# A longer lead loop in a two-layer attention and expert kernel: 16 more attention steps before the first expert tile, half A's post chain between its steps, expert scores computed token-major

## The reference, cut to what matters

```
x = x + tanh(g_xattn[0]) * attention0(layernorm(x), ctx)    # 16 heads of 16; 1024 queries x 1024 keys, quantized
x = x + tanh(g_ffn[0])   * experts0(layernorm(x))           # 32 experts of 176 units and a shared one of 352
x = x + tanh(g_xattn[1]) * attention1(layernorm(x), ctx)    # small
x = x + tanh(g_ffn[1])   * experts1(layernorm(x))           # 32 experts of 96 units, shared 192
```

```
scores = sigmoid(x @ router_weight.T)       # 32 experts
sfc = scores + e_bias                       # 8 groups of 4; the 4 groups whose two best sum highest stay
top 8 of what stays; combine = scores of those 8 / their sum * 2.5
```

## Time and profile before

| | |
|---|---|
| median of 3 runs | 980.28 us (980.24 to 982.89) |
| the profiled execution's own time | 977.45 us |
| its span in the profile | 975.7 us (1.75 us lie around it) |
| PE busy, weight loads, DVE, ACT, POOL | 878.6, 656.2, 760.2, 532.4, 574.2 us |
| mean granted PE clock | 0.948 |
| the chain that ended last | PE 65%, DVE 9%, POOL 6%, DMA 5%, issue 3%, ACT 3% |

### The profile page before, as it was taken

How to read it: one execution, slowest core, us unless ns; L and a number is a source line. 1 busy time by engine, 2 the same in 40 slices (tenths; PEclk the granted TensorE clock), 3 DMA queues, 4 the chain that set the end, 5 groups by cost and what they waited for, 6 DMA issues and landing times.

```text
span 975.7 us, 16764 instructions
## 1 busy us (share of the span) xinstructions
PE 878.6 (90%) x6100; PEld 656.2 (67%) x6100; DVE 760.2 (78%) x1058; ACT 532.4 (55%) x936; POOL 574.2 (59%) x500
## 2 busy tenths in 40 slices
PE   5627777877999999999899999999999999999997
PEld 4525445545777777777676777777776777777775
DVE  5998788665888888877777677878878767878886
ACT  4527777644666666655446645444446654343432
POOL 4433766655899898976586565444347554334341
PEclk9868788678999999999999999999999999999999
DMA  5006999832776666642222122323322112232320
GB/s 192 2 1 136 179 176 164 160 97 55 145 152 143 142 152 151 148 125 68 78 66 81 51 66 83 95 86 94 97 82 82 57 58 82 82 91 87 97 87 22
DMA packets 162083, 97.79 MB, mean 100 GB/s; under 512 B 138833, under 2 KB 142801, under 8 KB 162001
## 3 DMA queue, kind: packets, MB, share of 16 engines
q1 hardware_dynamic: 161728, 96.19, 40.2%
q10 hardware_dynamic: 272, 0.52, 0.1%
HBM read 62.08 MB, written 1.05 MB: 65 GB/s over the span
## 4 chain that ended last, share of the span: by engine, by line
PE 65%; DVE 9%; POOL 6%; DMA 5%; issue 3%; ACT 3%; DVEq 0%; SPq 0%; POOLq 0%; ACTq 0%
PE psum L226 19%; PE psum L228 18%; PE psum L227 18%; DMA pT<-p 5%; PE psum L736 3%; DVE qstack L1441 2%; ACT e L1036 2%; POOL p L1491 2%; POOL wlo L1499 2%; PE psum L907 1%; PE psum L746 1%; PE psum L747 1%; DVE qstack L1427 1%; PE psum L893 1%; DVE nmax L1185 1%
## 5 line engine op out<-in xcount | busy, mean ns | idle before, releaser
L1499 POOL TENSOR_TENSOR wlo<-wraw,whi 128x768 fp32r<-128x768 f32 x146 | 272.2, 1864 | 196.9 <-ACT whi L1046 194.9
L226 PE MATMUL psum<-actT_hi,whi 128*128 128x512 f32 x584 | 244.3, 418 | 4.0 <-issue 2.1
L1148 ACT ACTIVATE h_hi<-qstack 128x512 fp32r<-128x512 f32 x146 | 92.5, 633 | 260.6 <-DVE qstack L1441 244.2
L228 PE MATMUL psum<-actT_hi,wlo 128*128 128x512 f32 x584 | 233.0, 399 | 0.0
L227 PE MATMUL psum<-actT_lo,whi 128*128 128x512 f32 x584 | 232.7, 398 | 0.0
L1441 DVE TENSOR_TENSOR qstack<-qstack 128x512 f32<-128x512 f32 x136 | 184.5, 1357 | 12.5 <-DVE qstack L1427 0.5
L1491 POOL TENSOR_SCALAR p<-e 128x1024 f16<-128x1024 f32 x128 | 142.7, 1115 | 84.4 <-ACT e L1036 68.7
L1036 ACT ACTIVATE e<-psum,nmax 128x1024 f32<-128x1024 f32 x128 | 142.6, 1115 | 42.7 <-DVE nmax L1185 28.7
L1185 DVE TENSOR_REDUCE nmax<-psum 128x1 f32<-128x1024 f32 x128 | 152.8, 1216 | 14.7 <-PE psum L736 12.1
L1419 DVE SCALAR_TENSOR_TENSOR qstack<-qstack,psum 128x512 f32<-128x512 f32 x146 | 99.8, 684 | 66.0 <-ACT qstack L1111 65.4
L226 PEld LDWEIGHTS psum<-actT_hi,whi 128*128 128x128 f32 x584 | 111.0, 190 | 36.5 <-issue 6.2
(11 more groups left out here) (196 smaller groups left out, 1148.0 us busy)
## 6 DMA issues: line engine op xcount, KB each, us to landing
wraw<-in_wffn SPq DMA_DIRECT2D x146, 384.0 KB, 3.1
pT<-p SPq DMA_TRANSPOSE x128, 2.9
ctxT<-in_ctxT SPq DMA_DIRECT2D x2, 512.0 KB, 5.1
x<-in_x SPq DMA_DIRECT2D x1, 1024.0 KB, 8.5
ctok<-in_ctx SPq DMA_DIRECT2D x1, 1024.0 KB, 11.1
out<-x SPq DMA_DIRECT2D x4, 256.0 KB, 2.9
kstack<-in_Wkv ACTq DMA_DIRECT2D x1, 512.0 KB, 5.0
kstack<-in_Wq SPq DMA_DIRECT2D x1, 256.0 KB, 8.7
```

The source lines that it names most:

```text
L226: pe.matmul(out, l_hi, r_hi, start=start, stop=False, **kw)
L228: return pe.matmul(out, l_lo, r_hi, start=False, stop=stop, **kw)
L1499: pool.tensor_tensor(wlo[:, g % RING, :], wraw[:, g % RING, :], whi[:, g % RING, :].bitcast(F32), ALU.subtract).then_inc(cf["w_lo"], 1)
```

## The change

- The lead loop is 16 steps longer: `LEAD_OUT` = 80 steps are attended in it, `LEAD` = 84 are scored. There is no bridge.
- The post chain of half A's second unit stands between the loop's steps (70 to 82), like the first unit's. `weights_hi`/`weights_lo` for tiles 0 and 1 stand at s = 58 and 62.
- `paced()` starts at step 84 and puts two steps beside one tile of three and one beside the other two; `END0` becomes 38.
- `route(r)` makes its scores token-major for all four rounds: activations are now the stationary operand and the router's 32 columns the moving one, so there are 24 matmuls of 32 columns, each with a load of 128 columns. `route_sb`, `scores_transposed` and the copy out of PSUM go; tanh writes `score` and `score_in` works in place.
- `route0`'s part j of round 0 runs at the start of tile j on DVE, ahead of its s_g.
- `down(0)` waits for the tanh and for `osb`; `gate` of the first pass waits for exp of step 81.

```diff
-        LEAD = A_STEPS + LAG
-        BRIDGE = 4
+        LEAD_OUT = A_STEPS + HEADS0
+        LEAD = LEAD_OUT + LAG
...
-            s, out, j = LEAD + BRIDGE, LEAD + BRIDGE - LAG, QUIET
+            s, out, j = LEAD, LEAD_OUT, QUIET
             while out < STEPS:
-                n = 1 if j % 3 == 1 else 2
+                n = 2 if j % 3 == 0 else 1
...
                 def route(r):
                     pe.wait_ge(cp["x_lo"], 2 * r + 2)
-                    ps = bank(post_bank(r, 0, "route"))[0:EXPERTS, :]
-                    cut, layer = cols(r % 2), r // 2
-                    for k in range(KD):
-                        last = mm3(pe, ps, rw_hi[:, layer, k, :], rw_lo[:, layer, k, :], actT_hi[:, k, cut],
-                                   actT_lo[:, k, cut], start=k == 0, stop=k == KD - 1)
+                    ps, layer = bank(post_bank(r, 0, "route")), r // 2
+                    for t in range(TH):
+                        tt = slice((r % 2 * TH + t) * P, (r % 2 * TH + t + 1) * P)
+                        for k in range(KD):
+                            last = mm3(pe, ps[:, t * EXPERTS:(t + 1) * EXPERTS], actT_hi[:, k, tt], actT_lo[:, k, tt],
+                                       rw_hi[:, layer, k, :], rw_lo[:, layer, k, :], start=k == 0, stop=k == KD - 1)
...
                     if f == 0:
                         pe.wait_ge(c2["part"], made_before(j))
-                        pe.wait_ge(c2["exp"], LEAD)
+                        pe.wait_ge(c2["exp"], LEAD - 2)
...
                     if g == 0:
-                        pe.wait_ge(cp["score"], 1)
+                        pe.wait_ge(cp["route_sb"], 1)
+                        pe.wait_ge(c2["osb"], TH + 1)
...
-                    if s == 39:
-                        o_transposed(0, 0)
-                    elif s == 43:
-                        project(0, 0)
-                    elif s == 51:
-                        x_transposed(0, 0)
+                    if s in (39, 70):
+                        o_transposed(0, s > A_STEPS)
+                    elif s in (43, 73):
+                        project(0, s > A_STEPS)
+                    elif s in (51, 78):
+                        x_transposed(0, s > A_STEPS)
+                    elif s == 81:
+                        route(0)
...
 ACT
+                    if s in (40, 71):
+                        o_high(0, s > A_STEPS)
+                    elif s in (49, 77):
+                        norm_apply(act, ...)
+                    elif s in (52, 79):
+                        x_high(0, s > A_STEPS)
+                    elif s in (58, 62):
+                        weights_hi((s - 58) // 4)
+                    elif s == 82:
+                        route_act(0)
...
 DVE
+                    if s in (42, 73):
+                        o_low(0, s > A_STEPS)
+                    elif s in (46, 75):
+                        post_x(0, s > A_STEPS)
+                    elif s in (55, 81):
+                        x_low(0, s > A_STEPS)
+                out_lead(TH)
...
+                    if f == 0 and j < 3:
+                        route0(j, 0)
...
 POOL
+                    if s in (47, 75):
+                        norm_rstd(pool, ...)
+                    elif s in (58, 62):
+                        weights_lo((s - 58) // 4)
```

More of the change, by code:

```diff
@@ L613, in made_before @@
         def made_before(j):
-            return BRIDGE + sum(1 for i in AT if i < j and AT[i])
+            return sum(1 for i in AT if i < j and AT[i])
         def s_bank(s):
-            return 2 + 2 * (s % S_RING) if s < LEAD else 4 + 2 * ((s + 1) % 2)
+            return 2 + 2 * (s % S_RING) if s < LEAD else 4 + 2 * (s % 2)
         def s_user(s):
@@ L675, in post_bank @@
         def post_bank(r, u, stage):
-            return 1 if r == 0 else {"o": 4 + u, "y": 6 + u, "x": 4 + u, "route": 6, "score": 7}[stage]
+            return 1 if r == 0 else {"o": 4 + u, "y": 6 + u, "x": 4 + u, "route": 6}[stage]
         def tile_of(r, u):
@@ L704, in _ @@
                     load(g)
-                for s in range(LEAD + BRIDGE):
+                for s in range(LEAD):
                     turn(s)
@@ L902, in turn1 @@
                         pe.wait_ge(cx["pT_a"], n)
+                        if p == 0:
+                            pe.wait_ge(cp["route_sb"], half + 2)
                     else:
@@ L915, in attend1 @@
                     pe.wait_ge(cx["pT_d"], 2 * t + 2)
-                    if i == 0:
-                        pe.wait_ge(cp["score"], half + 2)
-                    else:
+                    if i > 0:
                         pe.wait_ge(cx["x"], t)
@@ L1001, in _ @@
                         attend(s - LAG, bank(0)[:, at:at + HD0])
-                o_transposed(0, 1)
-                scores(LEAD)
-                pe.wait_ge(c2["exp"], LEAD - 1)
-                attend_group([LEAD - LAG])
-                project(0, 1)
-                for i in range(1, BRIDGE):
-                    if i == BRIDGE - 1:
-                        x_transposed(0, 1)
-                    scores(LEAD + i)
-                    pe.wait_ge(c2["part"], i)
-                    attend_group([LEAD + i - LAG])
-                route(0)
                 for f in range(len(PASSES)):
@@ L1065, in route_act @@
                     act.wait_ge(cp["route_ps"], r + 1)
-                    act.activation(route_sb[0:EXPERTS, :], bank(post_bank(r, 0, "route"))[0:EXPERTS, :], ACT.Tanh,
-                                   scale=0.5).then_inc(cp["route_sb"], 1)
+                    if r > 0:
+                        act.wait_ge(cp["comb"], r)
+                    act.activation(score[:, :, :],
+                                   bank(post_bank(r, 0, "route"))[:, 0:TH * EXPERTS].rearrange("p (t e) -> p t e", t=TH),
+                                   ACT.Tanh, scale=0.5).then_inc(cp["route_sb"], 1)
                 def exp1(half, p):
@@ L1456, in _ @@
                         out_lead(s // HEADS0 - 1)
-                    if s == 42:
-                        o_low(0, 0)
-                    elif s == 46:
-                        post_x(0, 0)
-                    elif s == 54 + 1:
-                        x_low(0, 0)
-                out_lead(TH - 1)
-                row_max(LEAD)
-                o_low(0, 1)
-                out_group(GROUPS0[0][1])
-                row_max(LEAD + 1)
-                post_x(0, 1)
-                out_group(GROUPS0[1][1])
-                row_max(LEAD + 2)
-                out_group(GROUPS0[2][1])
-                x_low(0, 1)
-                row_max(LEAD + 3)
-                out_group(GROUPS0[3][1])
+                    if s in (42, 73):
[5 more added lines that the diff above has]
+                out_lead(TH)
                 for f in range(len(PASSES)):
@@ L1567, in _ @@
                     quantize(s)
-                    if s == 47:
-                        norm_rstd(pool, step, tile_of(0, 0), norm_at(0, 0), cn["stats"], cn["rstd"])
-                quantize(LEAD)
-                weights_lo(0)
-                quantize(LEAD + 1)
-                norm_rstd(pool, step, tile_of(0, 1), norm_at(0, 1), cn["stats"], cn["rstd"])
-                quantize(LEAD + 2)
-                weights_lo(1)
-                quantize(LEAD + 3)
+                    if s in (47, 75):
+                        norm_rstd(pool, step, tile_of(0, s > A_STEPS), norm_at(0, s > A_STEPS), cn["stats"], cn["rstd"])
+                    elif s in (58, 62):
+                        weights_lo((s - 58) // 4)
                 for f in range(len(PASSES)):
```

48 lines of the change are left out of this document (7 added, 41 removed).

## The result

The changed kernel takes 990.8 us (median of 5 runs, 987.65 to 993.97), the kernel before beside it 980.28 (979.28 to 982.89): ratio 1.0109, 95% interval 1.0083 to 1.0136. It is 1.1% slower. The forecast was 976.6, the range 971.0 to 984.0.

What follows compares the result with a forecast made beforehand. It took PE to bound the paced tiles, DMA to pace the lead loop, and waits to fill the bridge and tiles 0 to 2. Terms +8.4 - 9.9 - 5.3 + 3.1 = -3.7 us gave 976.6 us, range 971.0 to 984.0.

Steps and rivals of the forecast that it cites:

- Term 1: Lead loop against bridge: 16 more loop steps plus inserted work take 29.3 us instead of 20.9, +8.4 us.
- (a): Lead loop: route(0) ahead of attends 77 to 79, 2.8 us on PE, of which 0.8 exposed.
- (b): Lead loop: weight splits at s = 58 and 62 delay quantize; 3 us together with the second post chain.
- (c): Lead loop: tighter second post chain makes DVE wait 1 to 2.5 us; 3 us together with the weight splits.
- Term 2: Paced tiles: twelve steps fewer at 0.82 us of PE each, no other engine becoming the bound, -9.9 us.
- Term 3: Tiles 0 to 2: choice parts ahead of s_g, first gate to tile 3's 18.0 us instead of 23.3, -5.3 us.
- Term 4: Token-major scores in rounds 1 to 3: 24 matmuls in 2.8 us instead of 1.77, +3.1 us.
- rival C: Route matmuls: small moving operands don't hide the weight load, 4.6 us a route, 983.7 us; chance 0.12.
- B: Lead loop laid bare at post_x and weights_lo: inserts cost 12.6 us instead of 3, 986.2 us; chance 0.12.
- from 218 on: Sign at the lead loop's end: first gate matmul at 218 us or later, against about 213.9 forecast.
- the clock dropping in the longer loop: Lead loop sign of a wrong forecast: route and gate double in length at half speed.

Runs made afterwards that it cites:

- h1: The changed kernel with POOL's weights_lo behind h_lo in the paced tiles alone; 985.4 us, ratio 1.0049.
- e3: The kernel before with the weight splits of tiles 0 and 1 at s = 58 and 62 of the lead loop; 981.2 us, ratio 1.0031.
- e4: The changed kernel with the old form of the scores in all rounds; 983.6 us, ratio 1.0041.
- f2: The changed kernel with the eight unlift matmuls left out of each attend in the paced tiles, output wrong by the lift; 988.5 us, ratio 1.0084.
- f1: The kernel before with the choice's parts ahead of s_g in tiles 0 to 2, old scores; 979.6 us, ratio 1.0005.
- h2: e4 with a later second post chain, splits at steps 80 and 82, and weights_lo behind h_lo in the paced tiles alone; 975.7 us, ratio 0.9949.
- g2: The kernel before with POOL's order quantize, h_lo, weights_lo in all the first pass's tiles; 990.4 us, ratio 1.0103.
- e2: The kernel before with token-major scores and the choice's parts ahead of s_g in tiles 0 to 2; 991.5 us, ratio 1.0119.
- g1: The changed kernel with POOL's order quantize, h_lo, weights_lo in all the first pass's tiles; 997.7 us, ratio 1.0180.

## Why the prediction was wrong

The profiled execution came 16.5 us later where the sum said -3.7, a miss of 20.2 us; by the medians it is +10.5 and 14.2. The terms below are read from the two profiled executions and miss by 8.1, 5.5, 2.1 and 2.3 us; 1.7 are the later exp 0, and the rest lies between a gate and its s_g. Some 6 us of the 20.2 belong to these two executions and not to the kernels, the 1.7 among them; h1, with the same lead, was 4.0 us shorter from exp 67 to s_g 0.

**Term 1, the lead loop, is the step that failed most.** Up to the first gate the change costs 3.1 + 13.4 = 16.5 us, not 8.4. What was inserted cost 11.9 us for the 3.8 of the sum. (a) "I take 0.8 exposed" for `route(0)`, "2.8 the upper". It took 5.1 us, since the clock was at half there, and 4.5 of them were exposed. The price came from a row at the full clock for a stretch where the bridge shows 0.53. And the wait that was to hide it, "these attends wait for their transposes anyway", was over at 218.9 us, 1.5 us behind `route(0)`'s start. (b) and (c) "I take 3 us". The splits cost 2.3 to 3.1 and lie ahead of exp 67. The held-up transposes, which were to hide 2 to 3 us ("about 2", while its sum gives 3), hid little of them: two splits of 1.82 us cost 3.3 in e3. From exp 67 to exp 79 (212.25) it took 22.8 us where 12 steps of 1.54 are 18.5: 4.3 for the post chain, 3.8 of them at exp 76 (5.3 - 1.5; in e4, f2 and h1 it was 2.3). The chain's wait, foreseen as "1 to 2.5 us", was 2.64 of DVE's idle time, and `post_x` itself comes on top. The pace of 1.54 us for a step without inserts was right.

**Term 2, the paced tiles: "PE has no idle time there to swallow this" was wrong.** -4.4 came of the -9.9. A step was priced a little low, 0.82 us for 0.93 (17.20 less 16.28, one step). But with twelve steps fewer PE no longer bounds the stage: POOL's `weights_lo` against DVE's h does, by 0.62 us in three tiles. With POOL's order turned round the same twelve steps give -11.3 (205.9 to 194.6). The prediction named the lock for the choice alone, and h, at a mean of 1.64 us in the three tiles of the earlier trace rows, isn't among its rows. That row by itself would only have warned: in the kernel before, the stretched h cost nothing. The reading of the stage before, bound by PE, was right; that it would stay so was taken from the busy time of POOL and DVE, not from which of their operations stand ahead of s_g.

**Term 3, tiles 0 to 2:** -3.2 by the gates (20.1 for 23.3) instead of -5.3. The mechanism was right, with the race a tile later than foreseen: part 1's product, at the start of tile 1, met `weights_lo(3)`, began 0.01 us behind it and took 1.98 us. In h1 it was ahead, took 1.27 us, and tile 3's gate came 17.6 us behind tile 0's (17.2 from s_g to s_g). So the forecast's 17.2 and 19.0 were 17.6 and 20.1, the latter with PE's 1.11 us wait for the weights on top.

**Term 4, token-major scores:** the size of the 24 matmuls was right (2.70 us for 2.8), rival C (4.6) is out. In the changed kernel rounds 1 to 3 cost 5.4 us for 3.1. Rounds 2 and 3 account for 3.8: 2 x 0.9 for the matmuls, 1.5 for a half clock behind round 3's, which the prediction put at nothing, and 0.4 in tile 95, at neither burst. Seven kernels with bursts of 24 have 351.2 to 355.9 us from tile 50 to 118, three with bursts of 12 349.5 to 349.7, eight with the old scores 348.9 to 349.3 (the kernel before among them).

**The rivals.** B pointed the right way ("laid bare", 986.2), with the place half right: `post_x` yes, but a `route(0)` at half clock that holds the gate up by 4.5 us stood in no rival. The signs given for a wrong forecast, first gate "from 218 on" (it came at 223.8) and the clock dropping in the longer loop, both came true. The chance of slower, 0.20, was too small: terms 1 and 4 both rested on matmuls priced at full clock, term 2 on a busy share.

**What stays open.** Why the granted clock falls at different places of the lead loop in different executions, and what decides whether a burst is followed by a half clock: of the 14 bursts of 24 in rounds 2 and 3 of the seven traces 9 were (in the changed kernel round 3's, not round 2's), and 3 of the 7 in round 1; none of the 9 pairs of 12 and none of the 24 old ones. That a longer lead pays by itself isn't shown either. f1 with the short one and the old order of POOL is at 979.6 (ratio 1.0005), h2 with the long one at 975.7 (0.9949); they differ in POOL's order in the paced tiles too, and there that order gave nothing to the kernel before (g2), but the short lead was not run with it in those tiles alone.

## What to carry to other kernels

A PE that is busy in every slice need not be the bound. Count its work by the spacing of the matmuls' starts and compare with the stage's length; where the two differ, look for an elementwise instruction that takes two or three times its own shortest duration beside one of POOL. An operation that is stretched can cost nothing while PE has work queued, and start to cost when that work is taken away. Before a step is moved into a loop, list on every engine what is queued behind it and behind the waits that it brings (here the attends of steps 77 to 79 behind `route(0)`, row_max of step 76 behind `post_x`), see which of these the next stage waits for, and price it at the clock of the place that it goes to, not of the place where its row was read. An order of POOL that is right in one stage can be wrong in the next: weights_lo last gained 6.9 us in the paced tiles and lost 6 to 8 behind them, and only the versions that turned it in the one stage won.

## What the runs showed of the hardware that I had not expected

24 matmuls of 32 moving columns in a row, 2.70 us at full clock, were in 12 of 21 cases (rounds 1 to 3) followed by the lower clock, which in some set in with the burst's last matmuls (e2, g1, h1: up to 3.39 us for the 24). The next large matmuls were 0.43 us apart instead of 0.23, though the profile shows no idle time of PE (8.47 of 8.47 us busy, clock 0.80). One such fall cost 1.5 us, in h1 3.1 at round 3 (tile 114: 10.30 us for 7.17 in f2). The same 24 in two bursts of 12 with large matmuls between them left the clock at 1.00 in all 9 cases. A busy PE thus doesn't keep its clock by being busy in the profile.

The lead loop ran at anything between full and half clock from one execution to the next, with the same instructions up to there: `route(0)` took 5.1 us in the changed kernel's and 2.7 in h1's, and the runs of one kernel spread by 1.4 us (g2, 4 runs) to 13.6 (f2, 12 runs).
